# A two-layer decoder on one core: coupled network staggered between the batches, projections moved into second cross attention and to the opening of a pass, feed-forward reordered

## The reference

```python
x = ln(x + attn0(x))          # 16 heads of 64, softmax
x = ln(x + xattn0(x, ctx))    # 16 heads of 16, softmax
x = ln(x + ffn0(x))           # quantized: down(silu(gate(x)) * up(x)), 1024 wide
x = ln(x + attn1(x))          # gated linear attention, then an MLP of 768
x = ln(x + xattn1(x, ctx))    # keys and values K1, K2; softmax over the queries; z0, relu, z1
x = ln(x + ffn1(x))           # the coupled network
# ffn1:
gf = sigmoid(net3(x.mean(tokens)))                 # 256-128-64-1, "global"
for _ in range(3):                                 # three cycles
    tf = sigmoid(net4(out))                        # 256-256-128-64-1
    coupling = 0.1 + range_ * (0.7 * gf + 0.3 * tf - 0.5) * 2
    out = out + coupling * twist(out)
```

## Time and profile before

| | |
|---|---|
| three runs, median | 1389.76 us (1384.79 to 1397.29) |
| the profiled execution, its own time | 1389.56 us |
| its span, first to last instruction | 1387.8 us |
| instructions | 18027 |
| TensorE / VectorE / ScalarE / GpSimd busy | 84% / 55% / 48% / 23% of the span |
| mean granted clock of TensorE | 0.90 |

### The profile page before, as it was taken

One profiled execution on the slowest core, in us unless ns is written; L12 is line 12 of the kernel. 1 busy time (PEld: TensorE's weight loads), 2 busy tenths in 40 slices (PEclk: granted clock), 3 DMA queues, 4 the chain that ended last, 5 costly groups with the idle time before them and its releaser, 6 DMA issues.

```text
span 1387.8 us, 18027 instructions
## 1 busy us (share of the span) xinstructions
PE 1168.1 (84%) x6458; PEld 759.4 (55%) x6458; DVE 768.8 (55%) x1799; ACT 668.5 (48%) x1746; POOL 320.8 (23%) x619
## 2 busy tenths in 40 slices
PE   6986997898889997898898998698988987687855
PEld 3464644664556644674465664485555664375443
DVE  0175376546647377355637458464555737754553
ACT  2466245357357354346446635345535724545522
POOL 1145301131116310132105520221112630131110
PEclk9999999998999999896799999997699999999567
DMA  9200400000000000000000000000000000000000
GB/s 246 94 9 11 128 1 1 1 0 1 16 0 24 16 1 1 0 1 1 16 0 23 1 16 1 0 1 1 1 0 0 17 1 1 1 0 1 1 0 16
DMA packets 29988, 22.67 MB, mean 16 GB/s; under 512 B 14476, under 2 KB 29260, under 8 KB 29772
## 3 DMA queue, kind: packets, MB, share of 16 engines
q1 hardware_dynamic: 29308, 19.93, 5.5%
q10 hardware_dynamic: 592, 1.59, 0.3%
HBM read 19.42 MB, written 2.10 MB: 16 GB/s over the span
## 4 chain that ended last, share of the span: by engine, by line
PE 65%; DVE 17%; ACT 10%; issue 4%; POOL 3%; DMA 1%; SPq 0%; POOLq 0%; DVEq 0%
PE PS L525 8%; PE PS L512 6%; PE PS L920 5%; PE PS L661 4%; PE PS L676 4%; PE PS L690 4%; PE PS L647 4%; PE PS L933 3%; PE PS L584 3%; PE PS L785 2%; PE PS L894 2%; DVE x_room L1566 2%; ACT work L1467 2%; PE PS L573 2%; POOL rstd L2059 2%
## 5 line engine op out<-in xcount | busy, mean ns | idle before, releaser
L2059 POOL TENSOR_TENSOR rstd<-var,minus_half 128x2 f32<-128x2 f32 x64 | 46.4, 725 | 508.6 <-DVE var L1560 508.3
L1467 ACT ACTIVATE work<-PS,nmax 120x256 f32<-120x256 f32 x256 | 118.1, 483 | 65.5 <-DVE nmax L1950 65.5
L1631 DVE TENSOR_REDUCE nmax<-PS 128x2 f32<-128x512 f32 x128 | 81.9, 684 | 87.9 <-PE PS L647 87.6
L1950 DVE TENSOR_REDUCE nmax<-PS 120x2 f32<-120x512 f32 x128 | 82.0, 685 | 87.0 <-PE PS L920 86.7
L2071 POOL TENSOR_SCALAR work<-work,inv 128x256 f32<-128x256 f32 x256 | 126.8, 515 | 0.0
L2054 POOL TENSOR_TENSOR pool_pause<-minus_half 128x1 f32<-128x1 f32 x96 | 30.3, 316 | 399.8 <-DVE inv L1638 278.6
L1275 ACT ACTIVATE work<-PS,nmax 128x256 f32<-128x256 f32 x256 | 118.2, 482 | 8.9 <-DVE nmax L1631 8.8
L920 PE MATMUL PS<-x_room 32*120 32x256 f32 x512 | 89.1, 533 | 14.5 <-ACT work L1467 13.5
L647 PE MATMUL PS<-work 64*128 64x256 f32 x512 | 78.1, 425 | 16.4 <-ACT work L1275 15.6
L920 PEld LDWEIGHTS PS<-x_room 32*120 32x120 f32 x512 | 52.8, 243 | 48.0 <-issue 38.2
L661 PE MATMUL PS<-ident,work 128*128 128x128 f32 x512 | 72.8, 287 | 7.0 <-POOL work L2071 7.0
(11 more groups left out here) (267 smaller groups left out, 2509.3 us busy)
## 6 DMA issues: line engine op xcount, KB each, us to landing
x_room<-in_x_dram SPq DMA_DIRECT2D x4, 512.0 KB, 4.2
xa<-in_x_dram SPq DMA_DIRECT2D x4, 512.0 KB, 3.9
out_dram<-x_room SPq DMA_DIRECT2D x4, 512.0 KB, 3.1
rows<-in_rows_dram ACTq DMA_DIRECT2D x1, 1536.0 KB, 8.6
late<-in_L_attn_W_dram SPq DMA_DIRECT2D x2, 768.0 KB, 6.9
wv<-in_L_attn_kernel_dram SPq DMA_DIRECT2D x2, 512.0 KB, 9.2
wq<-in_L_attn_kernel_dram SPq DMA_DIRECT2D x2, 512.0 KB, 9.4
wk<-in_L_attn_kernel_dram SPq DMA_DIRECT2D x2, 512.0 KB, 7.7
```

What stands on the lines that cost most here:

```text
L1467: op = act.activation(e1[:, par, r, kv, :], bank(SCORE_1[r])[0:M, kv * S:(kv + 1) * S], ACT.Exp, bias=nmax1[:, par, r, kv:kv + 1], accum_o ...
L1950: dve.tensor_reduce(nmax1[:, par, r, :], bank(SCORE_1[r])[0:M, :].rearrange("p (v s) -> p v s", v=2), AX.X, ALU.max, negate=True).then_inc ...
```

## The change

The coupled network runs in four steps of pairs (batch, cycle), so that batch 1 is one cycle behind batch 0:

```diff
+    STEPS = (((0, 0),), ((1, 0), (0, 1)), ((1, 1), (0, 2)), ((1, 2),))
...
-        KEY_FILL = (7, 5, 7, 5, 7, 5, 7, 7)
+        KEY_FILL = (7, 7, 7, 7, 5, 7, 5, 7)
```

On TensorE:

```diff
+            def coupled_ffn(it, then=None):
+                for step in STEPS:
+                    for b, r in step:
+                        if r == 0:
+                            pe.wait_ge(x5_signed.sem, x5_signed.at(it, b + 1))
+                            turn(it, "c0", xs["5"], b)
+                        net_1(it, r, b)
+                        if r == 0:
+                            global_net_1(it, b, then)
+                    if step == STEPS[-1] and then is not None:
                         scores0(then, 0)
+                    for b, r in step:
+                        net_2(it, r, b)
+                        if r == 0:
+                            global_net_2(it, b)
+                    if step == STEPS[-1]:
+                        turn_final(it, 0, then)
+                    for b, r in step:
+                        net_3(it, r, b)
+                        if r == 0:
+                            global_net_3(it, b)
+                    for b, r in step:
+                        net_4(it, r, b)
...
             def attn0(it, last=None, then=None):
                 for u in range(U0 + 2):
+                    if last is not None and u == 0:
+                        keys0(it, J - 2)
                     if u + 1 < U0:
                         scores0(it, u + 1, last)
+                    if last is not None and u == 0:
+                        keys0(it, J - 1)
+                        turn_final(last, 1)
...
-                    if last is not None and u in (1, 2):
-                        turn_final(last, u - 1)
```

The global net runs for each batch by itself; ScalarE sums the tokens while it copies c0 (two activations with `accum_out`) and widens the second layer itself; the two VectorE instructions for that go. ScalarE and VectorE follow the same steps. ScalarE copies keys 6 and 7 behind `exp0(0)` and `exp0(1)`. VectorE:

```diff
+                for step in STEPS[:-1]:
+                    for b, r in step:
+                        couple(it, r, b)
                 if then is not None:
                     max0(then, 0)
+                sum_out(it, 0)
+                norm_summed(it, "out", 0)
+                couple(it, CYCLES - 1, 1)
...
-                    if last is not None and u in (5, 6):
-                        apply_norm(last, "out", of(res), y, u - 5)
-                    if last is not None and u in (4, 5):
-                        norm_summed(last, "out", u - 4)
-                    if last is not None and u in (2, 3):
-                        sum_out(last, u - 2)
+                    if last is not None and u == 1:
+                        apply_norm(last, "out", of(res), y, 0)
+                    if last is not None and u == 2:
+                        norm_summed(last, "out", 1)
+                    if last is not None and u == 3:
+                        apply_norm(last, "out", of(res), y, 1)
+                    if last is not None and u == 0:
+                        sum_out(last, 1)
```

Feed-forward, TensorE (ScalarE's copies of the context keys and of queries 1 and 2 move with it: `hidden_of(2)`, `context_keys(1)`, `keep_hidden(2)`, `keep_q0(1)`, `hidden_of(3)`, `keep_hidden(3)`, `keep_q0(2)`):

```diff
                 up(it, 1)
                 gate(it, 2)
+                up(it, 2)
                 turn_hidden(it, 0)
                 down(it, 0)
-                up(it, 2)
-                context1(it, 1)
                 gate(it, 3)
                 turn_hidden(it, 1)
+                up(it, 3)
                 down(it, 1)
-                up(it, 3)
+                context1(it, 1)
+                turn_hidden(it, 2)
                 if then is not None:
                     queries0(then, 1)
-                turn_hidden(it, 2)
                 down(it, 2)
+                turn_hidden(it, 3)
                 if then is not None:
                     queries0(then, 2)
-                turn_hidden(it, 3)
                 down(it, 3)
```

Second cross attention, TensorE (ScalarE: `keep_q0(7)` at n = 4, `keep_k0` 0 to 2 at n = 7, 11, 15):

```diff
                 queries_1(it, 0)
-                if then is not None:
-                    queries0(then, 7)
                 for n in range(0, GX * HC, 2):
                     scores_1(it, n)
                     if n == 2:
                         turn_normed(it, "x4", xs["4"], 1)
+                        if then is not None:
+                            queries0(then, 7)
                     if n == 6:
                         queries_1(it, 1)
+                    if then is not None and n in (6, 10, 14):
+                        keys0(then, (n - 6) // 4)
...
-                if then is not None:
-                    keys0(then, 0)
                 weigh_1(it, 2 * GX - 1)
-                if then is not None:
-                    keys0(then, 1)
                 turn_back(it, 1)
                 if then is not None:
-                    for j in (2, 3):
-                        keys0(then, j)
-                turn_normed(it, "z0", xs["z0"], 1)
+                    keys0(then, 3)
+                turn_normed(it, "z0", aff, 1)
```

More of the change, by code:

```diff
@@ L663, in turn0, with weigh0 @@
                     mm.then_inc(t0_done.sem, 1)
-            def weigh0(it, u):
+            def weigh0(it, u, last):
                 j, b = u // NB, u % NB
+                if u == 0 and last is not None:
+                    pe.wait_ge(summed["out"].sem, summed["out"].at(last, NB))
                 pe.wait_ge(t0_kept_v.sem, t0_kept_v.at(it, u + 1))
@@ L988, in turn_final, with net_2 @@
-            def turn_final(it, b):
+                    pe.wait_ge(kept["c0"].sem, kept["c0"].at(it, b + 1))
+                else:
+                    pe.wait_ge(st_done.sem, st_done.at(it, NB * (r - 1) + b + 1))
+                project_columns(n_w1, b, HIDDEN[b], turned_a if r == 0 else state[r - 1]).then_inc(hh1_done.sem, 1)
+            def net_2(it, r, b):
+                pe.wait_ge(hh1_kept.sem, hh1_kept.at(it, NB * r + b + 1))
+                for k in range(KD):
+                    mm = pe.matmul(bank(3 + b)[:, 0:S], n_w2[:, k, :], h1[:, k, b * S:(b + 1) * S],
+                                   start=(k == 0), stop=(k == KD - 1))
+                mm.then_inc(hh2_done.sem, 1)
@@ new lines, in global_net_1, with global_net_2 @@
+            def global_net_1(it, b, then):
+                pe.wait_ge(kept["c0"].sem, kept["c0"].at(it, b + 1))
+                if then is not None:
+                    pe.wait_ge(k0_kept.sem, k0_kept.at(then, 5))
+                for k in range(KD):
+                    mm = pe.matmul(bank(5)[:, b:b + 1], g_w1[:, k, :], gsum[:, k, b:b + 1], start=(k == 0), stop=(k == KD - 1))
+                mm.then_inc(gg1_done.sem, 1)
+            def global_net_2(it, b):
+                pe.wait_ge(gg1_kept.sem, gg1_kept.at(it, b + 1))
+                pe.matmul(bank(5)[0:G3, 2 + b:3 + b], g_w2[:, :], gh1[:, b:b + 1], start=True, stop=True).then_inc(gg2_done.sem, 1)
@@ L990, in turn_final @@
+            def turn_final(it, b, then=None):
+                n = (7, 6)[b]
                 pe.wait_ge(st_done.sem, st_done.at(it, CB - NB + b + 1))
-                if b > 0:
-                    pe.wait_ge(summed["out"].sem, summed["out"].at(it, b))
+                if b == 0 and then is not None:
+                    pe.wait_ge(k0_kept.sem, k0_kept.at(then, J - 2))
                 for ts in range(TS):
                     for c in range(KD):
-                        mm = pe.transpose(bank(7)[:, ts * D + c * P:ts * D + (c + 1) * P],
+                        mm = pe.transpose(bank(n)[:, ts * D + c * P:ts * D + (c + 1) * P],
@@ L1193, in one_pass @@
                 cross1(it, then)
-                for r in range(CYCLES):
-                    coupling_net(it, r, then)
+                coupled_ffn(it, then)
             pe.wait_ge(const_ready.sem, N_CONST)
@@ L1206, in _ @@
             one_pass(NI - 1, last=NI - 2)
-            for b in range(NB):
-                turn_final(NI - 1, b)
+            turn_final(NI - 1, 1)
         @blk.scalar
@@ L1295, in attn0 @@
                         exp0(it, u)
+                    if last is not None and u < 2:
+                        keep_k0(it, J - 2 + u)
                     if u >= 2 and u % 2 == 1:
@@ L1469, in cross1 @@
                     op.then_inc(p1_done.sem, 1)
+                    if then is not None and n in (7, 11, 15):
+                        keep_k0(then, (n - 7) // 4)
                     if n == GX // 2 * HC + 10:
-                        keep(it, "z0", 0, col["L1_xattn_g0"], col["L1_xattn_beta0"])
+                        keep(it, "z0", 0)
                 load_table(ACT.Gelu)
                 if then is not None:
-                    for j in range(4):
-                        keep_k0(then, j)
-                keep(it, "z0", 1, col["L1_xattn_g0"], col["L1_xattn_beta0"])
+                    keep_k0(then, 3)
+                keep(it, "z0", 1)
                 if then is not None:
@@ L2043, in _ @@
             one_pass(NI - 1, last=NI - 2)
[L2044 to L2047 removed]
+            apply_norm(NI - 1, "out", of(res), y, 0)
+            sum_out(NI - 1, 1)
+            norm_summed(NI - 1, "out", 1)
+            apply_norm(NI - 1, "out", of(res), y, 1)
         @blk.gpsimd
@@ L2065, in layer0 @@
             def layer0(it, last=None):
+                if last is not None:
+                    rstd_of(last, "out", 0)
                 for u in range(U0):
@@ L2073, in layer0 @@
```

(4 more changed lines are left out.)

283 lines of the change are left out of this document (131 added, 152 removed).

## The result

The changed kernel took 1333.81 us in the median of four runs (1332.72 to 1334.9), the kernel before 1387.85 us beside it: ratio 0.96, 95% interval 0.9551 to 0.9649. The forecast was 1335.6 us. The sum was right to 2 us, but two of its terms were far too large, one was far too small, and 8.5 us of the gain stood in no term.

A forecast was written before the change was run, and what follows sets the result against it. TensorE, busy 84% of the span, was taken as the bound, losing time only by standing still or at its lower clock. 1389.6 - 34.5 - 7 - 10.5 - 2 = 1335.6 us, range 1316 to 1362.

The forecast's parts named there:

- Feed-forward: Feed-forward stage of all four passes: reordered TensorE and ScalarE queues remove waits, gaining 34.5 us; bounds 26 and 38.
- the first piece: Feed-forward, third pass: with `up` issued earlier, VectorE does tiles 2 and 3 without a wait and ends 6.4 us earlier.
- Projections in the loop: Second cross attention: keys0 0 to 2 and queries0(7) moved into the score loop gain 7 us over three passes.
- the rest in six cases of ten: Score loop behind head 16, second and third passes: clock stays at 1.00 with chance 0.6, giving 4.6 us less 0.8.
- +1 with the first pass's clock: First pass's score loop: keys cost 3.3 us, covered waits and queries0(7) return 2.7, so about 1 us slower.
- z0 on VectorE and the sign 1.7 us earlier: End of second cross attention: moving z0's affine part from GpSimd brings the last sign from 1021.7 to 1020.0.
- Network and opening: Staggered network and next pass's opening: batch 0's first cycle fills a wait, 10.5 us gained over three passes.
- Fourth pass: Network of the fourth pass, without filler and low in clock: the last step gives back 6 us, net gain 2.
- C: Rival: feed-forward gains only part, queries0's one bank hands the wait on; 1365 us, chance 0.09.
- A: Rival: only the reordered feed-forward counts; loop and network cancel through falling clock; 1355 us, chance 0.20.
- D: Rival: batch 0's sparse first cycle sets 0.50 for every pass's network, 18.6 us each; 1449 us, chance 0.03.
- B: Rival: clock stays at 1.00 wherever TensorE is kept busy; loop 12, network 24, feed-forward 36; 1318 us, chance 0.10.

The follow-up runs named there:

- e1_ffn_only: The kernel before with only the feed-forward's new order on TensorE and ScalarE; 1351.3 us, ratio 0.9725.
- i2: The changed kernel with a fourth key projection, keys0(3), taken into the loop and the four keys at heads 10, 14, 18 and 22; 1315.52 us.
- e3: The changed kernel with keys0 0 to 2 behind the score loop and queries0(7) ahead of it again; 1338.84 us, ratio 0.9629.
- i4_keys_in_net: The changed kernel with keys0(6) and keys0(7) moved from the opening to behind the fourth layer of the network's two paired steps; 1325.48 us.
- e2_ffn_old: The changed kernel with the feed-forward's old order; 1362.69 us, ratio 0.9792.
- i1: The changed kernel with a fourth key projection, keys0(3), taken into the loop, keys at heads 6, 10, 14 and 18; 1343.6 us.
- b2: The changed kernel with keys at heads 10 to 22, keys0(6), (7) in paired network steps, keys0(4) earlier, and seven unread fourth-pass projections; 1295.86 us.

## Why the prediction was right, and where it wasn't

- **Feed-forward, 34.5 us forecast (10, 8.5, 9, 7):** 33.6 us in the traces (9.7, 8.0, 8.8, 7.1), and 35.0 between the medians for e1_ffn_only, whose stages alone give 33.2. The walk over both queues held: it had down(3) end 25.5 us after the first gate product (882.0 for 856.5), and it ends after 25.8. (By its own times VectorE's tile 3 ends 6.6 us earlier, not 6.4.) The vanished waits show that `up` ahead of the turn gives the first piece. That the rounding ahead of the copy gives the second is argued: no run separates the two.
- **Projections in the loop, 7 us forecast (+1, -3.5, -4.5):** 1.1 us (+4.4, -2.1, -3.4). What failed is the clock behind head 16, "the rest in six cases of ten", and "+1 with the first pass's clock": the clock was low there in all three passes, behind weigh_1(3) in the first and third and behind z0's turn in the second. The filled wait of 1.95 us came back two units further, as 1.81 us at weigh_1(3): I hadn't asked what is late next. "1.00 at least up to head 16" held in the first and third passes and not in the second (0.57 from 608 to 616), whose loop of 52.8 us is over the 52 that was named as a sign of being wrong. The price of the keys where the clock does the same was nearly right (1 to 1.8 us for 1).
  A reading was wrong too: the first pass did not go through the second half of the loop "at 1.00". Window of the kernel before:

```profile
332.00:344.00 12.00, 11.43 (x63) 6.52 (x65) 6.10 (x14) 6.77 (x27) 2.20 (x2) 0.57 0.01 2
```

  Of the 22.2 us from head 16 to the seventh weighing, 10 ran at 0.50. So 4.6 us a pass was not the price of the low level, and "1.00 throughout gives 12" was far too little: in i2, with one short dip in the third pass, the three loops take 129.8 us for 157.7 before, and with a fourth key in them. 8 to 10 us a pass lay in the keys' place.
- **z0 on VectorE and the sign 1.7 us earlier:** 1.6, 1.2 and 1.6 us, right. The apply pair of normalization 5 takes 0.73 us (L1615 at 976.83), where it took 2.70 beside GpSimd's two. With the keys out of the loop again (e3) about half of the gain is left (17.4 to 17.7 us from weighing to sign), so both edits have a share.
  The Trainium skill, "GPSIMD Engine Reference", section 8, names contention with VectorE instructions that have two SBUF inputs. Of the new affine instructions only the second pair (L1977) is of that kind; the first reads z0 from PSUM. No power of GpSimd runs beside the second pair, and the one beside the first (972.27) takes 0.69 us like most others. The one that takes 0.86 us (980.92) stands beside the centring of z1, as it did before (0.87), so the new instructions cost GpSimd nothing that the trace shows.
- **Network and opening, 10.5 us forecast for three passes:** 1.6 us. Opening 6.3 us and sign 4.4 us came; sign to tanh lost 9.1 (+3.9, +1.3, +3.9). The forecast's 0.8 a pass has the sign's 1.7 us in it, so it had taken a loss of 0.9 each, 2.7, from sign to tanh. The failed step is the sentence that TensorE's keys0 "only filled a gap that VectorE's 1.95 us sets". They did fill it only, but with the gap empty the first layer behind it ran wholly or in part at the low level in five of six handovers (all but the second one of the second pass). i4_keys_in_net puts them back, stays at 1.00 and has 31.8 us.
- **Fourth pass, 2 us forecast:** 9.7 us (sign 0.7, network 5.4, end 3.6). The kernel before had 37.3 us there, but e1_ffn_only, whose network is the old one, has 33.3: some 4 us are the clock's. I priced the single cycles at the low level, and they ran at 1.00 in this pass.
- **In no term:** 4.9 us between feed-forward and loop, 2.5 ahead of the feed-forward, 1.1 at the start. In e1_ffn_only the first of these stretches is 57.2, 57.2, 55.5 and 51.9 us, 5.8 less than before, and in e2_ffn_old, with the old order, 56.9, 60.1, 56.4 and 54.8, no less than before: the 4.9 come with the reordered feed-forward. Its upper end of 38 had named that.
- **Rivals.** C was refuted by e1. A's time of 1355 didn't come, though its mechanism, a clock that falls in the loop's second half and in the network, did. D's mechanism showed in two passes at 3.9 us and not 18.6. B, the clock at 1.00 wherever TensorE is kept busy, was wrong for this kernel: at 944 us it stays at 0.50 with 4.00 of 4.00 busy.
  The Trainium skill, "TensorE: Matmul & The Clock Gate", Part 1, says that idleness lowers the clock and matmul activity releases it. The falls in the middle of the loop and in the network agree with the first half (waits of 1.7 to 2.0 us stand there); those near head 6, with no wait over 1 us close ahead, don't show it. The second half doesn't hold for this loop: at 0.50 its instructions kept TensorE busy for all of the 20 us from 944 to 964, and the clock did not rise.

So the total was right partly by luck: 14.8 us too much in the loop and the network of passes 1 to 3, against 7.7 in the fourth pass and 8.5 in no term.

## What to carry to other kernels

When a filler is taken out of a gap that another engine sets, the gap's length is not its price: read what clock the instructions behind it get. Spread wide projections over a chain of narrow matmuls by its waits and not by their number, and look for the wait that filling the first one creates. Where a phase has no useful work left for its waits, work that no one reads can pay, if the phase behind it is filled as well: here 12 us of 1299 with both, and 3.4 with the first alone.

## What the runs showed of the hardware that I had not expected

- In one loop, with the same instructions, the clock is at 0.50 for 17 us in one pass and for 41 in the next (kernel before, 47.5 and 54.9 us). At 0.50 TensorE shows the higher busy time. Busy time is therefore no sign of a good clock.
- The falls in the loop's middle and in the network stand at a wait of 1.7 to 2.0 us. But a wait alone doesn't settle it: the changed kernel's second pass stays at 1.00 behind the 1.81 us of weigh_1(3) and behind the 1.91 us of its network's second handover, and there and in i1 the clock fell near head 6 with no wait over 1 us close ahead. Which of the two a pass gets stays open.
- The same projection, out_1(0) at 3.78 us, stands ahead of a rise of the clock in the loop before (993.83), and not after (958.12). What tells the two apart wasn't found.
- Projections that nobody reads cost little by themselves: in b2 the stretch ahead of the fourth pass's loop, with one of them, got 0.8 us longer (52.6 for 51.8), and the loop 10.5 us shorter with five inside it. What they did cost is 5.6 us in the network behind, by its clock.
